# Wide attention on one Trainium2 core: an item's two banks reduced one by one, every fourth sum on VectorE instead of every third, and the keys' low parts placed behind such a sum

## The chip, the cores and the metric

The kernel runs on one core of a Trainium2 chip. The metric is the device time of one execution in microseconds (us). Engines are named as the profile names them: PE (TensorE), DVE (VectorE), ACT (ScalarE), POOL (GpSimd), SP (SyncE, which issues the DMAs).

## What is computed

A decoder of two layers on 1024 tokens of width 128, with a context of 6404 rows of width 96. Layer 0: causal self-attention, cross-attention with 16 heads of 8, a mixture of experts. Layer 1: attention over the heads of each token, then the cross-attention that this change is about, then a mixture of experts. The reference of that cross-attention:

```
q = query @ w_q                  # 1024 x 128 by 128 x 1024
kv = context @ w_kv              # 6404 x 96 by 96 x 2048
k, v = jnp.split(kv, 2, axis=-1) # 16 heads of 64
scores = jnp.einsum('bhqd,bhkd->bhqk', q, k) * SCALE
attn = jax.nn.softmax(scores, axis=-1)
out = jnp.einsum('bhqk,bhkd->bhqd', attn, v)
return out.transpose(0, 2, 1, 3).reshape(B, NQ, INNER) @ w_out + b_out
```

## The kernel before

The stage is `wide_heads_and_experts`. The 16 heads are taken in 8 pairs, the 1024 queries in 2 halves: 16 units `n` (`UNITS`). A unit walks over `KT` = 51 tiles of 128 keys (the last has 4), tile `kt` of unit `n` being step `j = n * KT + kt`. All engines follow one list of steps, written out two steps at a time; two such steps are called a step pair here (j even, j + 1). `KT` is odd, so a tile that is the first of a step pair in an even unit is the second in an odd one.

In a step pair PE does, in this order: the scores of both steps (L2384: high part of keys by high part of queries, high by low, low by high, for two heads each, accumulated in PSUM banks 0 to 3); one maxima item (`early`); the weighing of the values with the probabilities of the two steps before (`weigh`, L2410); whole items (`whole`: keys `k`, queries `q`, sums `s`, output `y`, turned maxima `t`); the remaining maxima items (`late`), as a rule one. ACT turns scores into `prob` (L2537), a ring of 6 (`RING`).

A maxima item `m` (n, chunk, query tile) is for the unit after: PE multiplies bf16 queries by 512 bf16 keys for the pair's two heads (L2339), each head into a bank of its own, and DVE reduces each to one maximum per query. There are 52 such items a unit. The two banks come from a ring of three (5, 6, 7); an item takes the next two places, so the next item's second bank is this one's first. PE waits for both of its banks before the item. Where an item's banks lie side by side (5, 6 or 6, 7; `adjacent`), DVE takes both in one instruction (L2607), else in two (L2609).

```
def bank_of(item, s=0):
    return first_bank[item] + s if item in first_bank else SIDE + (place[item] + s) % BANKS
```

The sum of `prob` over the tiles is shared: POOL adds most tiles into `total` (L2259; tile 0 and 1 in one, L2255), DVE some from tile 7 on into `total_dve` (L2676; the first of a unit is a copy, L2673; the tile's name in the profile is k_xn, whose room it takes), chosen by `dve_adds(j)`. DVE adds a tile in the step pair after the one that made it, right behind the `early` maxima item. At a unit's end POOL folds the two (L2231). The sum's reciprocals (`invert`, L2648, four of 128 columns) are taken by DVE at tiles 11, 15, 19 and 23 of the next unit, and POOL scales the output with them (L2236).

Keys: a `k` item every sixth tile (tiles 3, 9, ..., 45 of even units, 3, ..., 27 of odd ones) makes 512 keys for the next pair of heads (PE L2357). ACT copies them twice (L2508, L2509), DVE subtracts the keys of 256 columns before (`k_step`, L2627), ACT rounds the difference to its high part (L2523, one step pair later) and DVE subtracts that, which leaves the low part (`leave_lo`, L2641, two step pairs later by `lo_of`).

DVE works its queue in order: early maxima item, sums, reciprocals, whole items, low parts, late maxima items.

Of the kernel before, what the change touches and what calls it, by code (L numbers as in the profile page):

```python
# [18 lines left out]
AX = mybir.AxisListType.X  # L19
# [8 lines left out]
KT = -(-NCTX // P)  # L28
# [55 lines left out]
def flat(t):  # L84
    return t.rearrange("p a b -> p (a b)")
# [1861 lines left out]
def wide_heads_and_experts(nc, name, net_name, PS, ident, ctxT, xn, xnT, x, O, A, values, out, wide):  # L1947
# [27 lines left out]
    QT = HALF // P  # L1975
# [3 lines left out]
    LAST = UNITS - 1  # L1979
# [5 lines left out]
    def slices(n):  # L1985

        return (11, 15, 19, 23) if n < LAST else (9, 11, 13, 15)
# [21 lines left out]
    tiled, whole, taken, turned = [], [], PER_UNIT, 1  # L2009
    for j in range(STEPS):  # L2010
        n, kt = j // KT, j % KT
        p = n // HALVES
# [23 lines left out]
    late = [items[1:] for items in tiled]  # L2036
    order = first + [item for items in zip(early, whole, late) for part in items for item in part] + last_items


    hi_of, lo_of = [[] for _ in range(STEPS // 2)], [[] for _ in range(STEPS // 2)]  # L2040
    for f in range(KF):
        if f >= 2:
# [3 lines left out]
    for r, items in enumerate(whole):  # L2046
        for item in items:
            if item[0] == "k":
                hi_of[r + 1].append(item)
                lo_of[r + 2].append(item)  # L2050
    first_hi, first_lo = [("k", 0, 0), ("k", 0, 1)], [("k", 0, 0)]
    hi_number = {item: i + 1 for i, item in enumerate(first_hi + [item for items in hi_of for item in items])}
    lo_number = {item: i + 1 for i, item in enumerate(first_lo + [item for items in lo_of for item in items])}
# [13 lines left out]
    first_bank, first_user = {("t", 0): PV}, {}  # L2067
# [34 lines left out]
    filled_count = {item: i + 1 for i, item in enumerate(order)}  # L2102


    def dve_adds(j):
        if j // KT == LAST:
            return j % KT % 2 == 1 and 7 <= j % KT
        return j % KT % 3 == 1 and 7 <= j % KT

    sum_count, by_pool, by_dve = [], 0, 0  # L2110
    for j in range(STEPS):
        by_pool, by_dve = by_pool + (not dve_adds(j)), by_dve + dve_adds(j)
# [2 lines left out]

    def bank_of(item, s=0):
        return first_bank[item] + s if item in first_bank else SIDE + (place[item] + s) % BANKS

    def adjacent(item):
        return bank_of(item, 1) == bank_of(item, 0) + 1  # L2120

    def value_slot(n, f):
        return (n * VF + f) % VBUFS
# [4 lines left out]
    def chunk(f):  # L2128
        return slice(f * HALF, min(NCTX, (f + 1) * HALF))
# [4 lines left out]
    with ExitStack() as stack:  # L2134
# [5 lines left out]
        top_piece, top = m.sb("top_piece", [P, 2, 2 * QT, MF]), m.sb("top", [P, QT, P])  # L2140
# [23 lines left out]
        side_filled, kept, dve_freed = m.sem("side_filled"), m.sem("kept"), m.sem("dve_freed")  # L2164
# [406 lines left out]
        def _(dve):  # L2571
# [6 lines left out]
            def side(item):  # L2578
                kind, n = item[0], item[1]
                if item in copy_number:  # L2580
                    c, qt = item[2:]
                    w = min(HALF, NCTX - c * HALF)
                    if c == 0:
                        return
                    i = merge_number[item]
                    dve.wait_ge(tile_copied, copy_number[item] + 1)
                    if c >= 2:
                        dve.wait_ge(tile_merged, i - (QT - 1) + 1)
                    now = run[qt - 1][:, :, 0:w]
                    dve.tensor_tensor(now, now, stage[i % SLOTS][:, :, 0:w], ALU.max).then_inc(tile_merged, 1)  # L2590
                    if c == MF - 1:
                        dve.wait_ge(tile_merged, i + 1)
                        dve.wait_ge(pieces_set, 1)
                        dve.tensor_reduce(top_piece[:, 0, :, :].rearrange("p (s t) c -> p s t c", s=2)[:, :, qt, 0],
                                          run[qt - 1], AX, ALU.max).then_inc(run_taken, 1)
                    if (c, qt) == (MF - 1, QT - 1):
                        dve.wait_ge(run_taken, QT - 1)
                        dve.wait_ge(dve_freed, dve_count["m", 0, MF - 1, 0, 1])
                        take_top(n)
                elif kind == "m":  # L2600
                    c, qt = item[2:]
                    w = min(HALF, NCTX - c * HALF)
                    dve.wait_ge(side_filled, filled_count[item])
                    pieces = top_piece[:, n % 2, :, :].rearrange("p (s t) c -> p s t c", s=2)
                    if adjacent(item):
                        b = bank_of(item)
                        dve.tensor_reduce(pieces[:, :, qt, c], PS[:, b:b + 2, 0:w], AX, ALU.max).then_inc(dve_freed, 2)  # L2607
                    for s in range(0 if adjacent(item) else 2):
                        dve.tensor_reduce(pieces[:, s, qt, c:c + 1], PS[:, bank_of(item, s), 0:w], AX,  # L2609
                                          ALU.max).then_inc(dve_freed, 1)  # L2610
                    if (c, qt) == (MF - 1, QT - 1):
                        dve.wait_ge(dve_freed, dve_count[item + (1,)])
                        if n >= 1:
                            dve.wait_ge(side_filled, filled_count[("t", n - 1)])
                        take_top(n)
                elif kind == "q":
                    dve.wait_ge(kept, hi_count[item])
                    dve.tensor_tensor(q_lo[n % QBUFS][:, :], PS[:, bank_of(item), :], q_hi[n % QBUFS][:, :].bitcast(F32),
                                      ALU.subtract).then_inc(dve_freed, 1)
                elif kind == "k":  # L2620
                    c = chunk(item[2])
                    lead = PAIR if item[2] == 0 else 0
                    dve.wait_ge(kept, hi_count[item])
                    if lead:
                        dve.tensor_copy(k_step[n % 2][:, 0:lead], PS[:, bank_of(item), 0:lead])
                    rest = slice(c.start + lead, c.stop)
                    dve.tensor_tensor(k_step[n % 2][:, rest], PS[:, bank_of(item), lead:c.stop - c.start],  # L2627
                                      k_raw[n % 2][:, rest], ALU.subtract).then_inc(dve_freed, 1)
                elif kind == "y":
                    dve.wait_ge(side_filled, filled_count[item])  # L2630
                    if n >= 1:
                        dve.wait_ge(dve_freed, dve_count[("y", n - 1)])
                    else:
                        dve.wait_ge(bias_added, 1)
                    rows = flat(x[:, n % HALVES * QT:(n % HALVES + 1) * QT, :])
                    dve.tensor_tensor(rows, rows, PS[:, bank_of(item), :], ALU.add).then_inc(dve_freed, 1)

            def leave_lo(item):
                c, p = chunk(item[2]), item[1]
                dve.wait_ge(hi_rounded, hi_number[item])  # L2640
                dve.tensor_tensor(k_lo[p % 2][:, c], k_step[p % 2][:, c], k_hi[p % 2][:, c].bitcast(F32),  # L2641
                                  ALU.subtract).then_inc(lo_left, 1)
# [7 lines left out]
            def copy_out(n):  # L2650
                dve.wait_ge(pv_done, (n + 1) * KT)
                if n >= 2:
                    dve.wait_ge(side_filled, filled_count[("y", n - 2)])
                dve.tensor_copy(outU[:, n % 2, :], PS[:, PV, :]).then_inc(out_copied, 1)
# [6 lines left out]
            for item in first:  # L2661
                side(item)
# [15 lines left out]
            for j in range(0, STEPS, 2):  # L2678
                for item in early[j // 2]:
                    side(item)  # L2680
                for i in (j - 2, j - 1):
                    if i >= 0 and dve_adds(i):
                        add(i)
                    if i >= 0 and i % KT == KT - 1:
                        copy_out(i // KT)
                for i in (j, j + 1):
                    if i >= KT and i % KT in slices(i // KT):
                        invert(i // KT - 1, slices(i // KT).index(i % KT))
                for item in whole[j // 2]:
                    side(item)  # L2690
                for item in lo_of[j // 2]:
                    leave_lo(item)
                for item in late[j // 2]:
                    side(item)
                if j // KT == LAST:
                    if j % KT == NET["center"]:

                        dve.wait_ge(scored, LAST * KT)
                        dve.wait_ge(dve_freed, dve_count[("y", LAST - 1)])
                        net.center(dve, 0, 0)  # L2700
                    if j % KT == NET["normalize"]:
                        net.normalize(dve, 0, 0)
                    if j % KT == NET["choose"]:
                        net.choose(dve, 0)
                    if j % KT == NET["gate"]:
                        net.gate(dve, 0)
                    if j % KT == NET["scale"]:
                        net.scale_input(dve, 0, 0)
# [309 lines left out]
```

## Time and profile before

| | us |
|---|---|
| median of 3 runs | 4040.47 |
| lowest, highest | 4039.4, 4046.2 |
| the profiled execution, its device time | 4047.36 |
| its span in the profile | 4045.6 |
| the steps of the stage, from 1690 to 3860 us of the span | 2170 |
| of these, about units 1 to 14, from 1836 to 3746 us | 1910 |

Shares of busy time tell how full an engine is, not what it waits for. For that the rows give, at each group of instructions, the idle time of its engine just before them and what ended it. The chain of waits is the work that ended last, followed back from the end. The mean granted TensorE clock of the execution was 0.955.

### The profile page before, as it was taken

To read this page: it belongs to the slowest core of one execution; us is meant where nothing else is said; L and a number is where in the kernel's file an instruction comes from. 1 tells how busy PE (TensorE), PEld (TensorE's weight loads), DVE (VectorE), ACT (ScalarE), POOL (GpSimd) and SP (SyncE) were. 2 spreads that over 40 slices of the span, in tenths; PEclk is the share of its full clock that TensorE was granted. 3 is DMA by queue.
4 is the path that set the end of the run, shared out by engine and by line. 5 is a ranking of instruction groups with operands and counts; after the bars stand their busy time and mean duration, and the time that the engine had idled before them with its cause. 6 is when DMAs were issued, how large, how long until landed. Compare 5 with 4: busy or idle time off the path is not lost.

```text
span 4045.6 us, 58225 instructions
## 1 busy us (share of the span) xinstructions
PE 3478.3 (86%) x21696; PEld 1341.8 (33%) x21696; DVE 3059.8 (76%) x4099; ACT 2266.4 (56%) x2759; POOL 2164.9 (54%) x1220
## 2 busy tenths in 40 slices
PE   6868999999998999778888888888888788888999
PEld 2332222222222344233333333333333333333444
DVE  6768888888887357777787778777878877788652
ACT  4658888888888546644444444444444444444532
POOL 3216565656564021256656666666667667667810
PEclk7969999999999999699999999999999999999999
DMA  4120010020001007000000000000000001002100
GB/s 126 50 49 1 1 27 8 1 34 2 1 1 49 4 11 266 6 21 24 28 24 25 26 24 27 24 25 26 25 25 28 24 25 29 24 23 92 34 3 6
DMA packets 74048, 126.54 MB, mean 31 GB/s; under 512 B 9875, under 2 KB 26341, under 8 KB 73093
## 3 DMA queue, kind: packets, MB, share of 16 engines
q1 hardware_dynamic: 73772, 122.82, 10.8%
q8 instruction: 178, 2.92, 0.3%
q14 instruction: 98, 0.80, 0.1%
HBM read 88.15 MB, written 34.64 MB: 30 GB/s over the span
## 4 chain that ended last, share of the span: by engine, by line
PE 55%; DVE 24%; issue 11%; ACT 3%; DMA 0%; SPq 0%; DVEq 0%; POOL 0%; ACTq 0%; POOLq 0%
PE PS L2410 12%; PE PS L1646 10%; DVE k_xn L2676 7%; PE PS L1591 6%; PE PS L2384 6%; DVE att_top_piece L2607 6%; PE PS L2339 5%; PE PS L1623 4%; DVE att_top_piece L1878 3%; DVE att_top_piece L2609 3%; PE PS L2357 2%; DVE att_k_lo L2641 2%; PE PS L546 1%; PE PS L340 1%; PE PS L559 1%
## 5 line engine op out<-in xcount | busy, mean ns | idle before, releaser
L2259 POOL TENSOR_TENSOR att_total<-att_total,att_prob 128x1024 f32<-128x1024 f32 (+1 forms) x537 | 1335.8, 2488 | 673.6 <-ACT att_prob L2537 643.2
L2537 ACT ACTIVATE att_prob<-PS 128x1024 f32<-128x1024 f32 x816 | 793.1, 1022 | 817.5 <-PE PS L2384 739.2
L1878 DVE TENSOR_REDUCE att_top_piece<-PS 128x1 f32<-128x512 f32 (+1 forms) x1459 | 905.0, 664 | 132.2 <-PE PS L1591 126.8
L1781 ACT ACTIVATE att_prob<-PS 128x1024 f32<-128x1024 f32 (+2 forms) x912 | 892.3, 1004 | 174.0 <-PE PS L1623 171.1
L2410 PE MATMUL PS<-att_prob,att_vals 128*64 128x512 f32 x3264 | 833.7, 633 | 3.6 <-issue 2.3
L2607 DVE TENSOR_REDUCE att_top_piece<-PS 128x2 f32<-128x1024 f32 (+1 forms) x533 | 628.9, 1180 | 202.7 <-PE PS L2339 198.4
L2339 PE MATMUL PS<-att_k_top,att_q_top 64*128 64x512 bf16 (+1 forms) x1664 | 334.3, 397 | 355.1 <-DVE att_top_piece L2607 259.1
L1646 PE MATMUL PS<-att_prob,cross_Vst 128*32 128x256 f32 (+1 forms) x5544 | 507.4, 432 | 1.9
L2676 DVE TENSOR_TENSOR k_xn<-k_xn,att_prob 128x1024 f32<-128x1024 f32 x231 | 496.4, 2149 | 11.9 <-ACT att_prob L2537 10.8
L2609 DVE TENSOR_REDUCE att_top_piece<-PS 128x1 f32<-128x512 f32 (+1 forms) x520 | 322.9, 662 | 123.3 <-PE PS L2339 122.9
L2384 PE MATMUL PS<-att_q_hi,att_k_hi 64*128 64x512 f32 x1632 | 402.1, 489 | 5.2 <-ACT att_prob L2537 3.2
L1493 POOL TENSOR_TENSOR att_stage<-att_stage,att_run 128x512 f32<-128x512 f32 x150 | 190.6, 1271 | 402.6 <-ACT att_stage L1760 402.4
L1591 PE MATMUL PS<-cross_Kstack,cross_Qmax 49*128 49x512 bf16 (+1 forms) x1664 | 323.5, 386 | 95.0 <-DVE att_top_piece L1878 33.0
L2339 PEld LDWEIGHTS PS<-att_k_top,att_q_top 64*128 64x128 bf16 x1664 | 90.8, 94 | 830.2 <-DVE att_top_piece L2607 447.8
L2384 PE MATMUL PS<-att_q_hi,att_k_lo 64*128 64x512 f32 x1632 | 328.0, 398 | 0.0
L2384 PE MATMUL PS<-att_q_lo,att_k_hi 64*128 64x512 f32 x1632 | 327.1, 397 | 0.0
L2410 PEld LDWEIGHTS PS<-att_prob,att_vals 128*64 128x64 f32 x3264 | 204.6, 141 | 348.9 <-issue 286.7
L1623 PE MATMUL PS<-cross_Qscore,cross_Kstack 49*128 49x512 bf16 x1632 | 309.0, 381 | 10.3 <-ACT att_prob L1781 6.0
L1591 PEld LDWEIGHTS PS<-cross_Kstack,cross_Qmax 49*128 49x128 bf16 x1664 | 100.4, 94 | 490.8 <-DVE att_top_piece L1878 341.2
L1495 POOL TENSOR_SCALAR att_stage<-att_stage 128x512 f32<-128x512 f32 x150 | 222.8, 1485 | 13.2
L2508 ACT ACTIVATE att_k_raw<-PS 128x512 f32<-128x512 f32 (+1 forms) x104 | 58.9, 567 | 296.7 <-PE PS L2357 296.7
L1646 PEld LDWEIGHTS PS<-att_prob,cross_Vst 128*32 128x32 f32 x5544 | 110.4, 108 | 275.4 <-ACT att_prob L1781 189.7
(322 smaller groups left out, 3625.0 us busy)
## 6 DMA issues: line engine op xcount, KB each, us to landing
att_vals<-values SPq DMA_DIRECT2D x192, 256.0 KB, 2.6
values<-att_prob SPq DMA_DIRECT2D x14, 1024.0 KB, 4.1
values<-cross_Vall SPq DMA_DIRECT2D x10, 1024.0 KB, 4.2
cross_Kstack<-kparts SPq DMA_DIRECT2D x36, 204.0 KB
f_w<-in_f_w SPq DMA_DIRECT2D x24, 256.0 KB, 3.5
kparts<-cross_Vst SPq DMA_DIRECT2D x24, 128.0 KB, 1.9
att_vals<-values SPq DMA_DIRECT2D x16, 192.0 KB, 2.3
k_ctxT<-in_ctxT SPq DMA_DIRECT2D x1, 2448.0 KB
```

Source lines behind the costliest of these rows:

```text
L1591: i = pe.matmul(PS[:, banks[item][s], 0:w], Qm[rows, g % 2, a, at:at + P], Kst[rows, g % 2, a, c * HALF:c * HALF + w], start=True, stop=Tr ...
L1623: i = pe.matmul(PS[:, 2 * (e % 2) + s, lo:HALF], Kst[rows, g % 2, a, kt * P:(kt + 1) * P], Qs[rows, g % 2, a, n % HALVES * HALF + lo:(n % ...
L1646: ins = pe.matmul(PS[r:r + 32, PV, lo:queries.stop], Vst[:, u % 2, kt, s, :], prob[:, j % RING, par, s, lo:queries.stop], start=(i == 0), ...
L1781: act.activation(prob[:, j % RING, par, :, lo:HALF], PS[:, 2 * (e % 2):2 * (e % 2) + 2, lo:HALF], ACT.Exp, scale=scale).then_inc(exped, 1)
L1878: dve.tensor_reduce(top_piece[:, n % 2, s * QT + qt, c:c + 1], PS[:, banks[item][s], 0:w], AX, ALU.max).then_inc(dve_freed, 1)
L2259: pool.tensor_tensor(so_far, so_far, prob[0:rows, j % RING, :, :], ALU.add).then_inc(summed, 1)
L2339: ins = pe.matmul(PS[:, bank_of(item, s), 0:w], q_top[strip(s), n % 2, qt * P:(qt + 1) * P], k_top[strip(s), c * HALF:c * HALF + w], start ...
L2384: i = pe.matmul(PS[:, b + s, :], k[p % 2][strip(s), keys], q[n % QBUFS][strip(s), :], start=kt < 2 and k is k_hi and q is q_hi, stop=last, ...
L2410: i = pe.matmul(PS[strip(s), PV, :], vals[:, value_slot(n, kt // 4), kt % 4, strip(s)], prob[:, j % RING, s, :], start=(kt == 0), stop=(kt ...
L2537: act.activation(prob[:, j % RING, :, :].rearrange("p a b -> p (a b)"), PSf[:, b:b + 2 * HALF], ACT.Exp, scale=scale).then_inc(exped, 1)
L2607: dve.tensor_reduce(pieces[:, :, qt, c], PS[:, b:b + 2, 0:w], AX, ALU.max).then_inc(dve_freed, 2)
L2676: dve.tensor_tensor(total_dve, total_dve, now, ALU.add).then_inc(dve_summed, 1)
```

## The change

Three things. An item's two banks are always reduced by two instructions (outside the first 13 items before step 0, which keep one). `dve_adds` gives DVE the tiles 7, 11, 15, ..., 47 of a unit, 11 in place of 15 (7, 10, ..., 49); the last unit keeps its rule. The low part of a `k` item is no longer taken two step pairs behind it wherever that falls, but in the first step pair from then on in which DVE adds a tile, and right behind that sum, ahead of reciprocals and whole items.

```
+    def dve_adds(j):
+        return j % KT % (2 if j // KT == LAST else 4) == (1 if j // KT == LAST else 3) and 7 <= j % KT
+
...
-                lo_of[r + 2].append(item)
+                lo_of[next(i for i in range(r + 2, r + 6) if dve_adds(2 * i - 2) or dve_adds(2 * i - 1))].append(item)
...
-    def dve_adds(j):
-        if j // KT == LAST:
-            return j % KT % 2 == 1 and 7 <= j % KT
-        return j % KT % 3 == 1 and 7 <= j % KT
-
...
-    def adjacent(item):
-        return bank_of(item, 1) == bank_of(item, 0) + 1
...
-                    pieces = top_piece[:, n % 2, :, :].rearrange("p (s t) c -> p s t c", s=2)
-                    if adjacent(item):
-                        b = bank_of(item)
-                        dve.tensor_reduce(pieces[:, :, qt, c], PS[:, b:b + 2, 0:w], AX, ALU.max).then_inc(dve_freed, 2)
-                    for s in range(0 if adjacent(item) else 2):
-                        dve.tensor_reduce(pieces[:, s, qt, c:c + 1], PS[:, bank_of(item, s), 0:w], AX,
+                    if item in first_bank:
+
+                        b = first_bank[item]
+                        dve.tensor_reduce(top_piece[:, 0, :, :].rearrange("p (s t) c -> p s t c", s=2)[:, :, qt, c],
+                                          PS[:, b:b + 2, 0:w], AX, ALU.max).then_inc(dve_freed, 2)
+                    for s in range(0 if item in first_bank else 2):
+                        dve.tensor_reduce(top_piece[:, n % 2, s * QT + qt, c:c + 1], PS[:, bank_of(item, s), 0:w], AX,
                                           ALU.max).then_inc(dve_freed, 1)
...
+                for item in lo_of[j // 2]:
+                    leave_lo(item)
                 for i in (j, j + 1):
                     if i >= KT and i % KT in slices(i // KT):
                         invert(i // KT - 1, slices(i // KT).index(i % KT))
-                for item in whole[j // 2]:
-                    side(item)
-                for item in lo_of[j // 2]:
-                    leave_lo(item)
-                for item in late[j // 2]:
+                for item in whole[j // 2] + late[j // 2]:
                     side(item)
```

PE's and ACT's instructions and their order are the same before and after.

DVE's queue in unit 2, from the sum of tile 10 to the first reciprocal behind the sum of tile 16, before (`k_xn` is the running sum on DVE):

```order
L2676 TENSOR_TENSOR k_xn<-k_xn,att_prob 128x1024
L2641 TENSOR_TENSOR att_k_lo<-att_k_step,att_k_hi 128x512
L2607 TENSOR_REDUCE att_top_piece<-PS 128x2
L2609 TENSOR_REDUCE att_top_piece<-PS 128x1 x2
L2676 TENSOR_TENSOR k_xn<-k_xn,att_prob 128x1024
L2648 RECIPROCAL att_sums<-att_sums 128x128
L2627 TENSOR_TENSOR att_k_step<-PS,att_k_raw 128x512
L2609 TENSOR_REDUCE att_top_piece<-PS 128x1 x2
L2607 TENSOR_REDUCE att_top_piece<-PS 128x2 x2
L2609 TENSOR_REDUCE att_top_piece<-PS 128x1 x2
L2676 TENSOR_TENSOR k_xn<-k_xn,att_prob 128x1024
L2648 RECIPROCAL att_sums<-att_sums 128x128
```

The same stretch of DVE's queue in the changed kernel, from the sum of tile 11 to that of tile 19 (its lines are numbered 4 to 5 lower; L2605 is a reduction of one bank):

```order
L2672 TENSOR_TENSOR k_xn<-k_xn,att_prob 128x1024
L2637 TENSOR_TENSOR att_k_lo<-att_k_step,att_k_hi 128x512
L2605 TENSOR_REDUCE att_top_piece<-PS 128x1 x4
L2644 RECIPROCAL att_sums<-att_sums 128x128
L2623 TENSOR_TENSOR att_k_step<-PS,att_k_raw 128x512
L2605 TENSOR_REDUCE att_top_piece<-PS 128x1 x4
L2672 TENSOR_TENSOR k_xn<-k_xn,att_prob 128x1024
L2605 TENSOR_REDUCE att_top_piece<-PS 128x1 x4
L2644 RECIPROCAL att_sums<-att_sums 128x128
L2614 TENSOR_TENSOR att_q_lo<-PS,att_q_hi 128x512
L2605 TENSOR_REDUCE att_top_piece<-PS 128x1 x4
L2672 TENSOR_TENSOR k_xn<-k_xn,att_prob 128x1024
```

Between two sums there are now four items' reductions (two rows of x4), the reciprocals stand in step pairs without a sum, and the key step behind tile 13's sum has no sum ahead of it any more.

POOL's queue over one unit in the middle, before (L2255 starts the sum with tiles 0 and 1, the row of 4x1024 is tile 50, L2231 the fold):

```order
L2255 TENSOR_TENSOR att_total<-att_prob 128x1024
L2259 TENSOR_TENSOR att_total<-att_total,att_prob 128x1024 x17
L2236 TENSOR_TENSOR k_O<-k_O,att_sums 128x512
L2259 TENSOR_TENSOR att_total<-att_total,att_prob 128x1024 x16
L2259 TENSOR_TENSOR att_total<-att_total,att_prob 4x1024
L2231 TENSOR_TENSOR att_total<-att_total,k_xn 128x1024
```

And in the changed kernel:

```order
L2250 TENSOR_TENSOR att_total<-att_prob 128x1024
L2254 TENSOR_TENSOR att_total<-att_total,att_prob 128x1024 x18
L2231 TENSOR_TENSOR k_O<-k_O,att_sums 128x512
L2254 TENSOR_TENSOR att_total<-att_total,att_prob 128x1024 x19
L2254 TENSOR_TENSOR att_total<-att_total,att_prob 4x1024
L2226 TENSOR_TENSOR att_total<-att_total,k_xn 128x1024
```

POOL has one more sum ahead of the scaling and three more behind it.

## Rows read from the trace of the kernel before

**Rows 1.** The page: span, and busy time of each engine.

```profile
span 4045.6 us, 58225 instructions
PE 3478.3 (86%) x21696; PEld 1341.8 (33%) x21696; DVE 3059.8 (76%) x4099; ACT 2266.4 (56%) x2759; POOL 2164.9 (54%) x1220
```

**Rows 2.** Windows: start:end, length, busy PE PEld DVE ACT POOL, PEclk, DMA, GB/s.

```profile
1836.00:3746.00 1910.00, 1595.32 (x9004) 689.37 (x9002) 1503.88 (x1469) 838.87 (x1010) 1253.79 (x527) 0.97 0.10 29
```

**Rows 3.** The chain that ended last, 1836 to 3746 us, by line.

```profile
by line: PE PS L2410 21.1%; issue 16.9%; DVE k_xn L2676 12.5%; DVE att_top_piece L2607 10.9%; PE PS L2384 10.6%; PE PS L2339 8.8%; DVE att_top_piece L2609 5.2%; PE PS L2357 3.4%; DVE att_k_lo L2641 2.6%; ACT att_k_top L2509 1.9%; DVE att_k_
```

**Rows 4.** Groups by line and form, 1836 to 3746 us: busy us, mean ns | idle before.

```profile
L2259 POOL TENSOR_TENSOR att_total<-att_total,att_prob 128x1024 f32<-128x1024 f32 x459 | 1132.4, 2467 | 585.7 <-ACT att_prob L2537 561.0 <-POOL att_total L2259 0.4
L2607 DVE TENSOR_REDUCE att_top_piece<-PS 128x2 f32<-128x1024 f32 x446 | 544.1, 1220 | 163.5 <-PE PS L2339 159.4
L2676 DVE TENSOR_TENSOR k_xn<-k_xn,att_prob 128x1024 f32<-128x1024 f32 x195 | 419.8, 2153 | 0.0
L2609 DVE TENSOR_REDUCE att_top_piece<-PS 128x1 f32<-128x512 f32 x446 | 285.9, 682 | 100.9 <-PE PS L2339 100.7
L2339 PE MATMUL PS<-att_k_top,att_q_top 64*128 64x512 bf16 x1338 | 268.4, 393 | 294.9 <-DVE att_top_piece L2607 218.7 <-DVE att_top_piece L2609 68.7 <-issue 2.8
L2641 DVE TENSOR_TENSOR att_k_lo<-att_k_step,att_k_hi 128x512 fp32r<-128x512 f32 x77 | 93.0, 1207 | 0.0
L2641 DVE TENSOR_TENSOR att_k_lo<-att_k_step,att_k_hi 128x260 fp32r<-128x260 f32 x7 | 15.2, 2176 | 0.0
L2339 PE MATMUL PS<-att_k_top,att_q_top 64*128 64x260 bf16 x110 | 15.7, 279 | 16.9 <-DVE att_top_piece L2607 13.1 <-DVE att_top_piece L2609 3.8
```

**Rows 5.** Timeline, unit 5, a step pair with keys and no sum: start us, us, engine.

```profile
2419.31 0.59 ACT L2509 ACTIVATE att_k_top<-PS 128x512 bf16<-128x512 f32 x1
2419.93 0.69 DVE L2627 TENSOR_TENSOR att_k_step<-PS,att_k_raw 128x512 f32<-128x512 f32 x1 [2.74 <-ACT att_k_top L2509]
2420.54 1.22 DVE L2607 TENSOR_REDUCE att_top_piece<-PS 128x2 f32<-128x1024 f32 x1
2421.86 0.39 PE L2339 MATMUL PS<-att_k_top,att_q_top 64*128 64x512 bf16 x2 [1.37 <-DVE att_top_piece L2607]
```

**Rows 6.** Timeline, unit 5, a step pair with keys, a sum and a reciprocal.

```profile
2451.88 2.40 DVE L2676 TENSOR_TENSOR k_xn<-k_xn,att_prob 128x1024 f32<-128x1024 f32 x1
...
2454.20 0.94 DVE L2648 RECIPROCAL att_sums<-att_sums 128x128 f32<-128x128 f32 x1
2455.07 0.62 DVE L2627 TENSOR_TENSOR att_k_step<-PS,att_k_raw 128x512 f32<-128x512 f32 x1
...
2456.92 0.39 PE L2339 MATMUL PS<-att_k_top,att_q_top 64*128 64x512 bf16 x2 [1.65 <-DVE att_top_piece L2607]
```

**Rows 7.** Timeline, unit 6, a sum, an output item and a low part behind it.

```profile
2625.31 2.35 POOL L2259 TENSOR_TENSOR att_total<-att_total,att_prob 128x1024 f32<-128x1024 f32 x1 [2.60 <-ACT att_prob L2537]
2626.35 2.40 DVE L2676 TENSOR_TENSOR k_xn<-k_xn,att_prob 128x1024 f32<-128x1024 f32 x1
2629.26 0.68 DVE L2641 TENSOR_TENSOR att_k_lo<-att_k_step,att_k_hi 128x512 fp32r<-128x512 f32 x1
2631.22 0.39 PE L2339 MATMUL PS<-att_k_top,att_q_top 64*128 64x512 bf16 x2 [1.48 <-DVE att_top_piece L2607]
```

**Rows 8.** Timeline, unit 7: a low part beside POOL's sum, later a split item.

```profile
2700.94 2.37 POOL L2259 TENSOR_TENSOR att_total<-att_total,att_prob 128x1024 f32<-128x1024 f32 x1 [0.44 <-ACT att_prob L2537]
2701.32 2.54 DVE L2641 TENSOR_TENSOR att_k_lo<-att_k_step,att_k_hi 128x512 fp32r<-128x512 f32 x1
...
2723.34 1.29 DVE L2609 TENSOR_REDUCE att_top_piece<-PS 128x1 f32<-128x512 f32 x2 [1.00 <-PE PS L2339]
```

**Rows 9.** All of line L2676: duration ns least/median/greatest.

```profile
L2676 DVE TENSOR_TENSOR k_xn<-k_xn,att_prob x231: 1214/2161/3411, 1721.3 to 3858.3; 128x1024 f32<-128x1024 f32 x116
```

## The prediction

> **What bounds the kernel now.** The shares come first, only to see who could be short: over the span DVE is busy 76% and PE 86% [rows 1], and in the stretch that holds units 1 to 14, 1910 us, PE is busy 1595 us, DVE 1504, POOL 1254 and ACT 839 [rows 2]. Nobody is full; PE is idle 315 us. The groups say where: 311.8 us of it stand before the maxima product L2339, of which 231.8 end with a combined reduction L2607 and 72.5 with a split one L2609 [rows 4]. So PE waits for PSUM banks that DVE has yet to reduce, and nearly nothing else. The chain of waits agrees: PE lines, the latencies between engines ("issue", 16.9%) and DVE in turn, with DVE's sums at 12.5%, its reductions at 16.1%, its low parts at 2.6% [rows 3]. POOL waits 561 us for ACT [rows 4]: it has room. The most that this change could win is those 312 us (and their like in unit 0), and whatever does not shorten the way to a free bank wins nothing.
>
> How a bank comes late is seen in the timeline. A sum on DVE takes 1.21 us where nothing stands against it, 2.16 as a median and up to 3.41 [rows 9]. In [rows 7] POOL's sum begins at 2625.31 and ends at 2627.66; DVE's sum begins at 2626.35 and ends at 2628.75, 1.09 after POOL's end: it did its work only once POOL was done. The low part in [rows 8] does the same: 2.54 us, ending 0.55 after POOL's sum, where one behind a sum of DVE takes 0.68 [rows 7]. Behind such a delay the late maxima item is reduced late, PE's next early item stands idle, 1.48 us in [rows 7].
>
> **The change, part by part.** Counts: per two units 30 sums become 22, 60 fewer in 15 units; the last unit is as before. Outside the first list 520 combined reductions (533 in all less 13) become 1040 single ones.
>
> A. Split items. The next item needs this one's first bank, and a split item gives it back after about 0.6 us, not 1.22. Both kinds stand in the trace: PE's idle time per combined item is 218.7/446 = 0.490 us, per split item 68.7/223 = 0.308 (446 instructions are 223 items); for the short last chunk 13.1/36 = 0.364 and 3.8/18 = 0.211 [rows 4]. So 446 x 0.182 + 36 x 0.153 = 86.8 us for 482 items, 94 for 520. Against it: two single reductions last 1.29 us together [rows 8], a combined one 1.22 to 1.23 [rows 4, 5], 0.06 x 520 = 31 us more on DVE, of which the share that reductions have on the chain counts (10.9% of 1910 = 208 of 569 busy, 0.37): 12. A = -82. Bounds: 0 (what I read as release is only where split items happen to stand) and -94.
>
> By the Trainium skill ("VectorE: DVE Perf Modes", the section on the TRN2 errata) a VectorE instruction with a PSUM source costs 120 cycles beside its elements; at 0.96 GHz that is 0.125 us for each added instruction, 65 us of DVE for 520, by an estimate from that page. The rows show half of it, 0.06, since the second reduction overlaps the end of the first; they decide. By the page A would be 82 + 12 - 24 = -70.
>
> B. Sums. On the chain they have 12.5% of 1910 = 239 us for 195, 1.22 each. They are not alike, though. In a step pair with keys DVE has to wait for ACT's second copy in any case: without a sum PE's next item stands 1.37 us [rows 5], with sum and reciprocal 1.65 [rows 6], so a sum there costs about 0.3. Counting from the tile numbers, 11 of the 30 sums of two units stood in key step pairs (7 and 4), and 6 of 22 do now (4 and 2); elsewhere it is 19 and 16. With 239 us for seven double units, 34.1 each, the others cost (34.1 - 11 x 0.3)/19 = 1.62. Gone are 3 x 1.62 + 5 x 0.3 = 6.4 per double unit, times 7.5: B = -48. Bounds -18 (60 at 0.3) and -97 (60 at 1.62).
>
> C. Reciprocals. Before, three of the eight of two units stood behind a sum in a step pair without keys; now none does, by the residues (3 mod 4 against a sum taken one pair after 3 mod 4). Next item behind one starts 0.87 us later (2455.07 less 2454.20 [rows 6]): 3 x 7.5 x 0.85 = 19. They now lie in the gap that a step pair without sum has, so C = -19; 0 if the gap isn't there.
>
> D. Low parts. 84 in the stretch took 108.2 us; at 0.68 (0.43 for the seven short ones, by their width) they would take 55 [rows 4, 7]. On the chain they have 2.6% = 50 us, 0.59 each [rows 3]. Now all come behind a sum or its copy; 6 of 13 fall in a step pair with keys and hide in DVE's wait, the rest cost some 0.6: 27 us left in the stretch. D = -25 with unit 0. Bounds 0 and -53.
>
> The Trainium skill ("SBUF — State Buffer", Who interferes with whom) says that GpSimd and a VectorE instruction with two SBUF inputs share a pair of ports, and that whoever is first blocks the other for its whole instruction. By that rule, the traces agree: the ends at +1.09 and +0.55 above. By it a low part right behind a sum finds the port still VectorE's, and no POOL sum gets between; but POOL's larger load would also stand before each remaining sum.
>
> E. POOL's load. It gets 60 sums of 2.47 us, 148 us, or 138 in the stretch, out of 585.7 us that it is idle before its sums [rows 4]; with the stretch shorter by some 120 it keeps about 330, so PE and ACT do not wait for it. But a DVE sum now always comes while POOL has both steps of the pair to add, two of 2.47 us in about 5.35 (1910 us over the 357 step pairs of 14 units). I take 0.25 us more per remaining sum (2.40 as in [rows 7] against 2.15) for 171 sums, with the chain's share of them, 1.22/2.15 = 0.57: E = +24. Bounds 0 and +122 (each as long as the greatest of [rows 9], 3.41, a sum that meets a POOL sum just begun: 97 us for each us of the mean, times 1.26).
>
> The terms of A overlap with the others: a delay that is gone cannot also be shortened. I take 15% off: (-82 -48 -19 -25 +24) = -150, less 22 = -128.
>
> Sum against the profiled execution: span 4045.6 - 128 = 3917.6; its device time is 1.8 above its span, 3919.4; and the median of the three runs lies 6.9 below the profiled execution's time: 3912.5. PE's clock dips (0.97 granted in the stretch [rows 2]) are left as they are.
>
> **Rivals.**
> 1. Only part of it comes through: PE's waits close in the step pairs with sums, but the split gives nothing (A at its bound 0, even +12), since the release was never what PE waited for. Then -48 -19 -25 +24 +12 = -56: 3984. For it: a mean over items that stand in different places isn't a comparison. Against: the 218.7 us are named by the trace as ended by L2607.
> 2. Slower: the remaining sums get longer by more than the rest wins. Place: DVE's sum behind the early item, with POOL's second sum of the pair already begun. The point: the gains A to D are 174 less overlap, about 150; at those 97 us for each us of mean length, the mean would have to rise from 2.15 to 3.7. At 4.0, if POOL also got in twice, +30: 4070. Against: that is above the longest of 231 sums, 3.41 [rows 9].
> 3. The split does not free PE but DVE's queue hides all: DVE is idle 400 us of 1910 [rows 2], so its work is taken off where it cost nothing; every gain and loss then ends within the noise, 4040. Against: the chain has DVE's lines in a third of the time.
> 4. More than forecast: no overlap, B at 1.62 for all, PE clock dips vanish with PE's idle stretches: -94 -97 -19 -53 = -263 as the end, 3830 to 3850 as likely size.
>
> **How the numbers follow.** Forecast, a gain of 60 to 190 us: 0.68. Rival 1 and its like, 10 to 60 us: 0.12. No change within 0.2% (8 us, about what a measurement here can tell): 0.04. Slower: 0.08. Larger gain: 0.08. Faster is 0.68 + 0.12 + 0.08 = 0.88. The predicted time is 3912; the range runs from 3850 (190 under the median) to 3990, into rival 1, and leaves out the larger gain and the slower cases, some 0.19.
>
> **What would show it.** In the changed profile: 1560 reductions of one bank and 171 sums; PE's idle time before the maxima product down from 312 to about 190 us in the same units, with the part per item at 0.3 or less (A); the low parts' mean at 0.68, none above 1 (D); no timeline with a reciprocal between a sum and a late item (C); the sums' mean at 2.2 to 2.5 (E); POOL's busy time up by about 148 us and still idle for ACT. Wrong would be: sums with a mean above 3 us, ACT's exponentials released by POOL's sums, or PE's idle time per item as before.

## The result, and the profile after

The changed kernel took 4144.64 us (4140.75 to 4146.02) beside 4043.34 for the kernel before, a ratio of 1.0249 with an interval of 1.0231 to 1.0267: 101 us slower, where 128 us faster was forecast. It lies outside the range of 3850 to 3990.

The page of the profile after, its first part (busy time), the clock line of the second, and the low parts' row of the costliest groups:

```profile
span 4144.3 us, 58225 instructions
PE 3533.8 (85%) x21696; PEld 1355.0 (33%) x21696; DVE 3129.3 (76%) x4559; ACT 2271.2 (55%) x2759; POOL 2389.2 (58%) x1280
PEclk7969999999999998788999989999999989999999
...
L2637 DVE TENSOR_TENSOR att_k_lo<-att_k_step,att_k_hi 128x512 fp32r<-128x512 f32 (+1 forms) x104 | 271.5, 2616 | 2.4 <-ACT att_k_hi L2518 2.4
```

The groups by line and form in the stretch that answers to [rows 4] (1862 to 3840 us, units 1 to 14; busy us, mean ns | idle before):

```profile
L2254 POOL TENSOR_TENSOR att_total<-att_total,att_prob 128x1024 f32<-128x1024 f32 x513 | 1333.4, 2599 | 469.0 <-ACT att_prob L2532 419.8 <-POOL att_total L2254 0.4
L2605 DVE TENSOR_REDUCE att_top_piece<-PS 128x1 f32<-128x512 f32 x1338 | 854.6, 683 | 216.3 <-PE PS L2334 214.2
L2672 DVE TENSOR_TENSOR k_xn<-k_xn,att_prob 128x1024 f32<-128x1024 f32 x139 | 306.7, 2207 | 0.0
L2334 PE MATMUL PS<-att_k_top,att_q_top 64*128 64x512 bf16 x1336 | 272.0, 401 | 327.7 <-DVE att_top_piece L2605 327.7
L2637 DVE TENSOR_TENSOR att_k_lo<-att_k_step,att_k_hi 128x512 fp32r<-128x512 f32 x77 | 212.5, 2760 | 0.0
L2637 DVE TENSOR_TENSOR att_k_lo<-att_k_step,att_k_hi 128x260 fp32r<-128x260 f32 x7 | 18.2, 2593 | 0.0
```

Beside [rows 4] one thing stands out. The 84 low parts of the stretch took 230.7 us where they took 108.2, 2.76 us each for the long ones; 0.68 was forecast. The sums' mean, 2.21, is as forecast, POOL still waits for ACT, and PE's idle time before the maxima product is 333.6 us (327.7 in the row shown and 5.9 of the short chunk), not the 190 of the forecast and more than the 311.8 before; an item has 0.46 us of it, and had 0.43.

The chain that ended last in the same stretch:

```profile
by line: PE PS L2405 24.9%; DVE k_xn L2672 12.5%; PE PS L2379 12.3%; DVE att_k_lo L2637 11.3%; DVE att_top_piece L2605 10.2%; PE PS L2334 8.3%; issue 6.1%; POOL att_total L2254 3.6%; PE PS L2352 2.7%; DVE att_k_step L2623 2.5%; ACT att_k_to
```

Against [rows 3] the low parts rose from 2.6% to 11.3%, and the latencies between engines fell from 16.9% to 6.1%: more of the chain is DVE's queue, and more is PE's weighing (24.9% against 21.1%). The timeline shows one such place, in unit 7, from the changed kernel's trace (start us, us):

```profile
2777.18 8.40 POOL L2254 TENSOR_TENSOR att_total<-att_total,att_prob 128x1024 f32<-128x1024 f32 x3 [4.91 <-ACT att_prob L2532]
...
2778.22 2.41 DVE L2672 TENSOR_TENSOR k_xn<-k_xn,att_prob 128x1024 f32<-128x1024 f32 x1
...
2780.55 2.82 DVE L2637 TENSOR_TENSOR att_k_lo<-att_k_step,att_k_hi 128x512 fp32r<-128x512 f32 x1
2783.30 2.54 DVE L2605 TENSOR_REDUCE att_top_piece<-PS 128x1 f32<-128x512 f32 x4
2784.13 0.39 PE L2334 MATMUL PS<-att_k_top,att_q_top 64*128 64x512 bf16 x2 [3.57 <-DVE att_top_piece L2605]
2784.45 3.42 PE L2405 MATMUL PS<-att_prob,att_vals 128*64 128x512 f32 x8
```

DVE's sum waits for POOL's first sum and ends at 2780.63. The low part is the next in DVE's queue, and yet it ends only at 2783.37, 2.74 later: one POOL sum (2.36, the median of its line in the trace before) and 0.4 of its own. POOL's second sum stood ready and went first. The late reductions come after 2783, and PE's early item stands 3.57 us. Then the eight weighing products take 3.42 us, at a granted clock of 0.55; the eight ahead of the stop, from 2776.90, took 1.94 at 1.00.

So PE lost time in two ways: it stood longer, and it worked more slowly. The windows over the whole stage, from 1690 us to its end, of the kernel before and of the changed one (length, busy PE PEld DVE ACT POOL, then PEclk):

```profile
1690.00:3856.00 2166.00, 1815.09 (x10201) 786.17 (x10201) 1689.92 (x1647) 960.85 (x1157) 1429.91 (x594) 0.97 0.10 29
```

```profile
1690.00:3955.00 2265.00, 1870.29 (x10207) 799.79 (x10203) 1759.94 (x2106) 966.68 (x1157) 1654.98 (x654) 0.93 0.10 27
```

PE does the same work in both, so 55 us more of busy time are its lower clock (0.93 against 0.97, between its two levels of 1.2 and 2.4 GHz), and the idle time, length less busy, rose from 351 to 395 us: 44. Together the 99 us of the stage. This is an account of where PE's time went. It doesn't show that 55 us would come back at the full clock, since a faster PE might only wait longer for DVE.

### The profile page after: what moved, and what is told of

Same layout as the page of the kernel before. It is cut to its first block, busy times and chain, and to the rows that moved or that the text cites. A ratio compares the mean times of both kernels' runs of the same rounds, so it can differ in the third digit from the quotient of the medians.

```text
span 4144.3 us, 58225 instructions
## 1 busy us (share of the span) xinstructions
PE 3533.8 (85%) x21696; PEld 1355.0 (33%) x21696; DVE 3129.3 (76%) x4559; ACT 2271.2 (55%) x2759; POOL 2389.2 (58%) x1280
## 4 chain that ended last, share of the span: by engine, by line
PE 56%; DVE 27%; issue 6%; ACT 3%; POOL 3%; DMA 0%; SPq 0%; DVEq 0%; POOLq 0%; ACTq 0%
PE PS L2405 13%; PE PS L1646 9%; PE PS L2379 7%; DVE k_xn L2672 7%; PE PS L1591 6%; DVE att_k_lo L2637 6%; DVE att_top_piece L2605 5%; PE PS L2334 5%; PE PS L1623 3%; DVE att_top_piece L1878 3%; POOL att_total L2254 2%; PE PS L2352 2%; PE PS L546 1%; PE PS L340 1%; PE PS L559 1%
## 5 line engine op out<-in xcount | busy, mean ns | idle before, releaser
L2254 POOL TENSOR_TENSOR att_total<-att_total,att_prob 128x1024 f32<-128x1024 f32 x597 | 1560.4, 2614 | 564.0 <-ACT att_prob L2532 506.2
L2605 DVE TENSOR_REDUCE att_top_piece<-PS 128x1 f32<-128x512 f32 (+1 forms) x1560 | 965.5, 663 | 275.1 <-PE PS L2334 271.8
L1878 DVE TENSOR_REDUCE att_top_piece<-PS 128x1 f32<-128x512 f32 (+1 forms) x1459 | 905.0, 664 | 131.1 <-PE PS L1591 125.6
L2405 PE MATMUL PS<-att_prob,att_vals 128*64 128x512 f32 x3264 | 886.7, 668 | 5.1 <-issue 4.2
L2672 DVE TENSOR_TENSOR k_xn<-k_xn,att_prob 128x1024 f32<-128x1024 f32 x171 | 374.5, 2190 | 8.4 <-ACT att_prob L2532 6.8
L2637 DVE TENSOR_TENSOR att_k_lo<-att_k_step,att_k_hi 128x512 fp32r<-128x512 f32 (+1 forms) x104 | 271.5, 2616 | 2.4 <-ACT att_k_hi L2518 2.4
```

The source lines that it names most:

```text
L1878: dve.tensor_reduce(top_piece[:, n % 2, s * QT + qt, c:c + 1], PS[:, banks[item][s], 0:w], AX, ALU.max).then_inc(dve_freed, 1)
L2254: pool.tensor_tensor(so_far, so_far, prob[0:rows, j % RING, :, :], ALU.add).then_inc(summed, 1)
L2405: i = pe.matmul(PS[strip(s), PV, :], vals[:, value_slot(n, kt // 4), kt % 4, strip(s)], prob[:, j % RING, s, :], start=(kt == 0), stop=(kt ...
L2605: dve.tensor_reduce(top_piece[:, n % 2, s * QT + qt, c:c + 1], PS[:, bank_of(item, s), 0:w], AX, ALU.max).then_inc(dve_freed, 1)
L2672: dve.tensor_tensor(total_dve, total_dve, now, ALU.add).then_inc(dve_summed, 1)
```

## The experiments

The theory after the result: POOL's waiting sum takes the port between DVE's sum and the low part. The rivals: the split itself costs; POOL's larger load costs, wherever the low parts stand.

### Each part alone, and two of them

The edits, on the kernel before: `split_only` makes `adjacent` true for the first items only; `sums4_only` changes the residue; `split_sums4` has both; `lo_only` takes the two edits of the low parts.

```diff
-        return bank_of(item, 1) == bank_of(item, 0) + 1
+        return item in first_bank
...
-        return j % KT % 3 == 1 and 7 <= j % KT
+        return j % KT % 4 == 3 and 7 <= j % KT
```

> Kernel before with only the split reductions. Theory (the low parts are what costs: POOL's waiting sum takes the port between DVE's sum and the low part): the split itself is harmless, PE's idle time per maxima item falls to about 0.3 us, time 3960 to 4000, 40 to 80 us under before. Rival (the split is what costs, two instructions an item on the path): 4060 to 4100 and PE's idle time per item as before or more.

Measured: 3904.27 us, ratio 0.9657 (0.9639 to 0.9675), 140 us faster. The split is no cost; it wins more than either theory said. The stage's window of this kernel:

```profile
1690.00:3723.00 2033.00, 1759.87 (x10215) 773.04 (x10215) 1722.24 (x2170) 962.59 (x1158) 1451.59 (x595) 0.99 0.11 30
```

Idle time falls from 351 to 273, by 78 us, and busy time by 55: the clock, 0.99 for 0.97. Before the maxima product PE stands 0.31 us an item (1840 to 3700 us), where it stood 0.43, as the theory said.

> Kernel before with only every fourth sum on DVE, low parts and reductions as before. Theory of the low parts: no more than a small effect, 3980 to 4040, though a low part that falls behind a sum whose pair is all POOL's is blocked here too (mean of the low parts between 1.2 and 2.2 us). Rival (POOL's larger load is what costs, wherever the low parts stand): 4100 or more, with the low parts' mean near 1.2.

Measured: 4171.65 us, ratio 1.0313 (1.0298 to 1.0329), 127 us slower. The low parts' new place was not in this kernel, so it is not the only cost. My theory's time failed; its aside did not. The low parts here (least/median/greatest ns of one):

```profile
L2641 DVE TENSOR_TENSOR att_k_lo<-att_k_step,att_k_hi x104: 628/1995/2849, 1677.0 to 3723.0; 128x512 fp32r<-128x512 f32 x96, 128x260 fp32r<-128x260 f32 x8
```

The median was 0.68 before and is 2.0 here. Their place in the list of steps is unchanged, but by the tile numbers 42 of the 91 in this stage's steps now come behind a sum in a step pair whose two tiles are both POOL's, and before none did. The 45 of the trace that start directly behind a sum take 2.64 us as a mean, the others 1.39.

> The changed kernel with the low parts put back to two step pairs behind their keys, behind reciprocals and whole items. Theory: the low parts' new place is the cost, so this is 100 us or more under the changed kernel: 3930 to 4020. Rival (POOL's load costs): within 30 us of the changed kernel, 4110 to 4150.

Measured: 4038.76 us, ratio 0.9983 (0.997 to 0.9995). That is 106 us under the changed kernel, as the theory asked, but 19 us above its bound, and 134 above the split alone. Its timeline in unit 5 is nearly that of the changed kernel, though no edit put the low part there: for the keys made at tiles 9, 21, 33 and 45 of even units and 9 and 21 of odd ones, two step pairs later is the pair of a sum.

```profile
2451.01 8.40 POOL L2259 TENSOR_TENSOR att_total<-att_total,att_prob 128x1024 f32<-128x1024 f32 x3 [1.55 <-ACT att_prob L2537]
2452.05 2.41 DVE L2676 TENSOR_TENSOR k_xn<-k_xn,att_prob 128x1024 f32<-128x1024 f32 x1
...
2454.38 2.82 DVE L2641 TENSOR_TENSOR att_k_lo<-att_k_step,att_k_hi 128x512 fp32r<-128x512 f32 x1
...
2457.95 0.39 PE L2339 MATMUL PS<-att_k_top,att_q_top 64*128 64x512 bf16 x2 [3.57 <-DVE att_top_piece L2609]
```

> Kernel before with only the low parts moved, right behind DVE's next sum, while DVE still adds every third tile. Theory: with every third tile the pair after the one that made DVE's tile mostly has only one tile for POOL, no sum of POOL waits when DVE's ends, so most low parts take 0.68 us (mean under 1.2) and the time is 3990 to 4040. Rival (a low part right behind a sum is always worse, since it lengthens the same delay): mean near 0.7 and yet 4050 to 4080. A second rival (the port always passes to POOL behind a DVE sum): mean near 2.6, 4100 to 4140.

Measured: 4059.61 us, ratio 1.0037 (1.0023 to 1.0051), 15 us slower. The low parts' median is 0.68 and the mean of the long ones 0.93 from 1840 to 3700 us, as the theory said of the port; the time was 20 us above its range and in that of the first rival. So low parts that are short gave no gain behind a sum. That they lengthen the delay there, as the rival says, is likely but not shown: the sums' mean rose as well, to 2.27 in the same window against 2.15, and what makes this kernel slower by 15 stays open.

### The port between the sum and the low part

> The changed kernel with one wait more: POOL's second sum of a step pair in which DVE takes a low part waits until that low part is done. Theory (POOL's waiting sum takes the port between DVE's sum and the low part, 2.1 us each for some 90 low parts, and PE's long stop behind it brings its clock down): the low parts' mean falls from 2.6 to under 1.2, the time falls by 150 us or more, to 3880 to 4000. Rival (POOL is the short engine with three sums of four): a wait more on POOL makes it slower, 4150 to 4200.

```diff
                 pool.wait_ge(exped, j + 1)
+                if j % 2 == 1 and lo_of[j // 2]:
+                    pool.wait_ge(lo_left, lo_number[lo_of[j // 2][-1]])
```

Measured: 3853.17 us, ratio 0.9525 (0.9505 to 0.9544), 291 us under the changed kernel from one wait more on POOL, and 194 under the kernel before. It beats both. The same place of unit 7 in its trace:

```profile
2609.31 2.36 POOL L2256 TENSOR_TENSOR att_total<-att_total,att_prob 128x1024 f32<-128x1024 f32 x1 [1.22 <-ACT att_prob L2534]
2610.35 2.40 DVE L2674 TENSOR_TENSOR k_xn<-k_xn,att_prob 128x1024 f32<-128x1024 f32 x1
...
2612.68 0.68 DVE L2639 TENSOR_TENSOR att_k_lo<-att_k_step,att_k_hi 128x512 fp32r<-128x512 f32 x1
2613.49 4.85 POOL L2256 TENSOR_TENSOR att_total<-att_total,att_prob 128x1024 f32<-128x1024 f32 x2 [1.82 <-DVE att_k_lo L2639]
2614.11 0.39 PE L2336 MATMUL PS<-att_k_top,att_q_top 64*128 64x512 bf16 x2 [1.42 <-DVE att_top_piece L2607]
2614.43 1.94 PE L2407 MATMUL PS<-att_prob,att_vals 128*64 128x512 f32 x8
```

The sum is as long as before; the low part takes 0.68 (0.72 as a mean of all, under the 1.2 of the theory), POOL stands 1.82 us for it, PE's stop is 1.42 instead of 3.57, and the weighing behind it runs at the full clock. In its stage PE idles 217 us and is busy 1746:

```profile
1690.00:3653.00 1963.00, 1746.09 (x10171) 768.71 (x10171) 1563.09 (x2099) 956.63 (x1151) 1565.07 (x652) 0.99 0.11 32
```

> The changed kernel with the low part directly ahead of DVE's sum, not behind it. Theory of the port: the second of the two is blocked whichever it is; the low part falls to a mean of 1.0 to 1.9, the sums of those pairs rise to about 3.4, both together about 5 us as before, and the time stays within 40 us of the changed kernel, 4100 to 4180. Rival (the low part is slow for another reason than what stands before it in the queue): the low parts keep a mean of 2.6.

The edit moves the loop over `lo_of` ahead of the loop that adds. Measured: 4147.79 us, ratio 1.0247 (1.0217 to 1.0276), the changed kernel's within the interval. Low part and sum have changed roles:

```profile
L2637 DVE TENSOR_TENSOR att_k_lo<-att_k_step,att_k_hi x104: 680/1877/2868, 1675.1 to 3689.5; 128x512 fp32r<-128x512 f32 x96, 128x260 fp32r<-128x260 f32 x8
L2672 DVE TENSOR_TENSOR k_xn<-k_xn,att_prob x171: 1210/3046/3410, 1721.8 to 3940.1; 128x1024 f32<-128x1024 f32 x171
```

The low parts' median fell from 2.83 to 1.88 us and the sums' rose from 2.41 to 3.05. The 80 pairs that follow each other directly took 5.05 us together, low part 1.82 and sum 3.22; in the changed kernel 80 such pairs took 5.03, sum 2.30 and low part 2.73. The first waits for the rest of POOL's sum, the second for a whole one; the low part has nothing slow of its own.

> The changed kernel with the low parts in the first later step pair in which DVE adds no tile. Theory (what costs is the sum and the blocked low part one behind the other, over 5 us): a low part alone waits for POOL at most 2.4 us, mean 1.5 to 2.6, and PE's next item is held back less, 3950 to 4040. Rival (the low part's own length is all that counts, wherever it stands): within 30 us of the changed kernel, 4110 to 4150.

```diff
-lo_of[next(i for i in range(r + 2, r + 6) if dve_adds(2 * i - 2) or dve_adds(2 * i - 1))].append(item)
+lo_of[next(i for i in range(r + 2, r + 6) if not (dve_adds(2 * i - 2) or dve_adds(2 * i - 1)))].append(item)
```

Measured: 3891.34 us, ratio 0.9626 (0.9607 to 0.9645), 253 us under the changed kernel and more than the theory said.

```profile
L2637 DVE TENSOR_TENSOR att_k_lo<-att_k_step,att_k_hi x104: 679/2558/2889, 1671.9 to 3446.9; 128x512 fp32r<-128x512 f32 x96, 128x260 fp32r<-128x260 f32 x8
```

```profile
1690.00:3697.00 2007.00, 1753.19 (x10171) 769.73 (x10167) 1698.81 (x2098) 956.06 (x1150) 1629.44 (x652) 0.99 0.11 31
```

The low parts are still long here, 2.56 us against 2.83 as a median, 2.06 against 2.62 as a mean. So it is not mainly their length that costs, but two blocked instructions in one step pair: apart, PE idles 254 us in the stage against 395, and the clock stays at 0.99. Against the kernel with the wait, 38 us remain.

### What is left of each part when the low parts are shielded

> Split reductions, every third sum on DVE as before, low parts right behind DVE's next sum, and POOL's second sum of that pair waits for them. Theory: every low part takes 0.7 us, none is blocked, so this is at or under the split alone: 3870 to 3910. Rival (the low parts right behind a sum lengthen a delay that a place elsewhere hides, as lo_only was 15 us slower than before): 3915 to 3950.

Measured: 3897.11 us, ratio 0.9634 (0.9618 to 0.9651), 7 us from the split alone, whose interval is 0.9639 to 0.9675: not to be told apart with confidence, and inside the theory's range. With every third sum there is little to shield: by the tile numbers 7 of the 91 low parts have a pair with two tiles of POOL's. Against the version above with every fourth sum, which differs in nothing else, it is 44 us slower.

> The version in which POOL waits for the low part, with every fifth sum on DVE (tiles 7, 12, ..., 47, nine a unit) in place of every fourth. Theory (a sum fewer is a stop fewer for PE as long as POOL has room): 3820 to 3850. Rival (POOL becomes the short engine: four sums of 2.5 us in five steps, with two blocked spells): 3870 to 3950, and ACT's exponentials or DVE's copy are released by POOL's sums.

Measured: 3879.12 us, ratio 0.9597 (0.9571 to 0.9623), 26 us above the version with every fourth sum. The rival was right in the time, not in its sign: from 1700 to 3600 us no sum of POOL is in the list of what ACT or DVE waited for. PE idles 237 us and is busy 1760, against 217 and 1746. What costs instead was not tried.

> The version in which POOL waits for the low part, with two neighbouring banks reduced in one instruction again. It measures the split by itself where no low part is blocked: if the early release of the first bank is what it gives, 100 to 150 us are lost, 3950 to 4000, and PE's idle time before the maxima product rises from 202 to about 300 us; if the split gave something only in company of blocked low parts, under 50 us are lost, below 3900.

The edit gives neighbouring banks one instruction again. Measured: 3993.02 us, ratio 0.986 (0.9844 to 0.9876). The split is worth 140 us here too.

```profile
1690.00:3804.00 2114.00, 1799.86 (x10189) 779.89 (x10189) 1548.78 (x1586) 960.02 (x1155) 1559.39 (x653) 0.97 0.10 29
```

Idle 314 against 217, busy 1800 against 1746: 97 us of waiting, 54 of clock.

### The clock

> The changed kernel with twelve more products of one head (results overwritten at once) between the free first bank and the awaited second bank of the early maxima item that follows a low part, so that PE is not idle there. Nothing else changes: the sum and the blocked low part stay as long. Theory (part of the cost is that PE's clock falls to half behind the long stops): the mean granted clock of the stretch rises from 0.93 to 0.96 or more, the time falls by 35 to 90 us, to 4055 to 4110, although PE does more. Rival (the lower clock costs nothing, since DVE is what the stage waits for): 4140 to 4200.

> As the kernel with twelve more products, with four, some 1.5 us, which is shorter than the stops behind the low parts, so that they add little of their own. Theory (PE's standing idle is what brings its clock down, and that costs): mean granted clock of the stretch 0.95 or more and time 4080 to 4130. Rival (the clock falls there whether PE has such work or not): clock 0.93 to 0.94 and time within 25 us of the changed kernel, 4120 to 4170.

```diff
+                    if item in held:
+                        for _ in range(FILL):
+                            pe.matmul(PS[:, bank_of(item), 0:w], q_top[strip(0), n % 2, qt * P:(qt + 1) * P],
+                                      k_top[strip(0), c * HALF:c * HALF + w], start=True, stop=True,
+                                      tile_position=(0, 0))
+                        wait_place(place[item] + 1)
```

`held` are the early maxima items of the step pairs right behind one with a low part. With twelve: 4242.15 us, ratio 1.0484 (1.0451 to 1.0518), outside both ranges. With four: 4129.25 us, ratio 1.0198 (1.0183 to 1.0213), 15 us under the changed kernel, inside both. The windows of the two, twelve first:

```profile
1690.00:4051.00 2361.00, 2109.44 (x11291) 889.67 (x11291) 1759.00 (x2103) 961.68 (x1153) 1650.64 (x652) 0.94 0.09 26
```

```profile
1690.00:3937.00 2247.00, 1926.82 (x10529) 817.41 (x10525) 1754.70 (x2095) 959.58 (x1149) 1646.94 (x651) 0.94 0.10 28
```

The mean clock stays at 0.94, as the rival said. But the edit did what it was meant to do in half of the places only. Two places of the kernel with twelve:

```profile
2782.39 2.76 PE L2337 MATMUL PS<-att_k_top,att_q_top 64*128 64x512 bf16 x12
2785.53 0.39 PE L2342 MATMUL PS<-att_k_top,att_q_top 64*128 64x512 bf16 x2 [0.37 <-DVE att_top_piece L2613]
2785.84 1.94 PE L2413 MATMUL PS<-att_prob,att_vals 128*64 128x512 f32 x8
```

```profile
2426.57 4.08 PE L2337 MATMUL PS<-att_k_top,att_q_top 64*128 64x512 bf16 x10 [2.46 <-DVE att_k_step L2631]
...
2431.86 2.88 PE L2413 MATMUL PS<-att_prob,att_vals 128*64 128x512 f32 x8
```

In the first the twelve products start at once and fill the stop. In the second a whole item had taken the first bank, which DVE had yet to free, so PE stood 2.46 us all the same and the twelve came on top. Of the 93 places 46 are of the first kind. There the weighing behind took over 2.5 us in 10, where it did so in 36 of the same 46 places of the changed kernel. In the other 47 it did so in 37, against 31. So light work that fills the stop did keep the clock up in most places; the mean hides it, because it takes in the other half. With four, some 1.0 us, PE still stood 2.3 us behind them, or 2.2 ahead of them, and in 63 of the 93 the weighing took over 2.5 us, against 67. What the lower clock costs in time stays open, as neither kernel took the stops away without adding work.

## Why the prediction was wrong

**What bounds the kernel** was right: PE waits for banks that DVE reduces late. The two kernels and the ten runs that left PE's work as it was stand in the same order by their time, 3853 to 4172 us, and by PE's idle time in the stage, 217 (`pool_waits_lo`) to 427 us (`sums4_only`). Between these two the stage differs by 327 us, 210 of them idle and 117 busy.

**Term A**, -82 net, was right in mechanism and too small, outside its own bound of -94: -140 alone, and 140 with the low parts shielded. Idle time fell by 78, nearly my number, and busy time by 55 through the clock, which I had left as it is. The 0.06 us per split that the rows gave did no visible harm.

**Term D** is the first step that failed, in the sentence that "a low part right behind a sum finds the port still VectorE's, and no POOL sum gets between". That one engine holds the port for a whole instruction is as the Trainium skill says ("SBUF — State Buffer", Who interferes with whom), and the traces agree (the ends 1.09 and 0.55 us behind POOL's). What comes at the end of an instruction the page doesn't say: that DVE keeps the port for its next one was my inference, from [rows 7], though the prediction gives it as following from the rule. In [rows 7] POOL had only one tile of the step pair: the pair is tiles 30 and 31, and 31 was DVE's. In the changed kernel every sum of DVE outside the last unit falls in a pair of two POOL tiles (the residue 3 mod 4, one pair later), and with it all 91 low parts, so one of POOL's sums always waits. In the kernel before none of the 91 did: each had a pair with one tile of POOL's, and its short low parts could not show what happens with two. I had used the pair of two in term E and not in D. The trace of before had a case with POOL's next work waiting, in unit 6, which I did not weigh:

```profile
2609.38 2.16 DVE L2676 TENSOR_TENSOR k_xn<-k_xn,att_prob 128x1024 f32<-128x1024 f32 x1
...
2610.40 2.27 POOL L2236 TENSOR_TENSOR k_O<-k_O,att_sums 128x512 f32<-128x512 f32 x1
...
2611.46 1.76 DVE L2641 TENSOR_TENSOR att_k_lo<-att_k_step,att_k_hi 128x512 fp32r<-128x512 f32 x1
```

POOL's scaling goes in between, and the low part takes 1.76. Forecast -25; on top of the other two parts it measured +106 (4038.76 to 4144.64), with low parts of 2.76 us where 0.68 was forecast.

**Terms B and C**, -48 and -19, had the wrong sign: +127 alone, +134 beside the split. With the low parts shielded, going from every third to every fourth sum gives -44, the forecast sign and two thirds of the size. So the loss again goes with unshielded low parts (their busy time rose by 76 us in the first, by 78 in the second); the price of a sum was one with the low parts at 1.2 us. Fewer sums on DVE is more on POOL's queue, and a step on POOL's queue is what blocks a low part. C was not measured apart from B.

**Term E**, +24, was sized on the wrong instruction: the sums' mean rose to 2.21 only (2.40 forecast), and in units 1 to 14 ACT never waited for POOL (6.5 us in the whole execution); its larger load came out in the low parts.

**The clock** was left as it is in the sum. In the account of PE's time it is 55 of the changed kernel's 99 us in the stage, and 55 of the split's 133; what it costs by itself is not shown.

**The rivals**: the slower one (0.08) named the sums with a mean of 3.7 as the place. The greatest sum is 3.44, and the mean hardly moved; the blocked low part behind it was the mechanism, with 5.2 us for the two. So that rival had the sign and POOL's second sum of the pair right, but not the instruction that it hits. That the parts do not add is the rest: split -140, sums +127, low parts +15 sum to +2; all three together are +101.

## What to carry to other kernels

- When two engines share a port, an instruction right behind another of the same engine is not sheltered: if the other engine has work waiting, it went first here. Look at what the other queue has ready at that moment, not at the duration of the instruction elsewhere; a wait on the other engine for the short instruction can be worth far more than it costs (here 291 us).
- A blocked instruction alone may hide for the most part; two in one stretch between two releases did not (253 us between the two placements here). Count delays per stretch, not per instruction.
- Where PE's idle spells get long, look at the clock too: its busy time for the same instructions shows it, before and after.
- When an experiment adds work to fill a stop, look in its trace where the work landed before reading its time: here half of it came behind the stop.

## What the runs showed of the hardware

The handover of the port: a low part took 0.68 us with nothing waiting on POOL and 2.83 as the median with a sum waiting, and it went both ways round (low part or sum second, 5.03 and 5.05 us for the two). PE's granted clock was 0.55 in the weighing behind a stop of 3.57 us, which took 3.42 instead of 1.94 us, and 1.00 behind one of 1.42. Where twelve bf16 products of one head filled such a stop, the weighing behind took over 2.5 us in 10 of 46 places, in place of 36.
